# A graph layer with a layer norm on one core: column groups of 7, 1, 7, 1 blocks in place of 6, 2, 6, 2, one drained block a step, three raw slots in place of four

## The chip, the cores and the metric

The kernel runs on one core of a Trainium2 chip. The metric is device time in microseconds (us) of one execution; lower is better.

## The reference

With x of 8192 x 128, a dense adjacency matrix adj of 8192 x 8192, W of 128 x 128 and b of 128, all float32:

```python
h = jnp.maximum(_layernorm(x, axis=-1), 0.0)
support = jnp.matmul(h, W)
out = jnp.matmul(adj, support) + b
return x + jax.nn.relu(out)
```

The kernel computes it as (adj h) W: for each output column block it sums h-transposed times adj-transposed over all 8192 nodes and then projects the sum with W.

## The kernel before

**Tiling.** The output, transposed to 128 features x 8192 nodes, is cut into 16 column blocks of 512 (one PSUM bank each). The contraction runs over 64 k-tiles of 128 nodes. The blocks are done in four groups (WIDTHS, line 16): 6, 2, 6 and 2 blocks wide, on PSUM banks 0 to 5, 6 and 7, 0 to 5, 6 and 7. Group g takes all 64 k-tiles before group g+1 begins. A step handles DEPTHS[g] k-tiles of a group: 1 in the wide groups, 3 in the narrow ones, so nearly every step has six pairs of k-tile and block. There are 64 + 22 + 64 + 22 = 172 steps; the narrow groups begin at steps 64 and 150, the last of each has one k-tile.

**One step.** SP loads the step's part of adj into a slot of `raw` (line 270). ACT copies it to `high` in the rounded type fp32r (line 404). DVE writes `low` = raw - high, the rest that the rounding left (line 543). PE makes three fp32r products for each pair of k-tile and block (line 585): h_high x high, h_low x high, h_high x low. They are summed in the block's bank. Only the first two steps (FOUR_PASS, line 627) are plain float32 products straight from `raw`, since their h isn't split yet.

**Slots.** There are 4 of `raw`, 3 of `high`, 2 of `low`. SP's load of step t waits until DVE has made `low` of step t - 4 (line 297; for steps 4 and 5 until PE has used the raw slot, line 294). ACT's `high` of step t waits for `low` and the last use of `high` of step t - 3 (lines 399, 400). DVE's `low` of step t waits for PE's last product of step t - 2 (line 539). A step's load is cut into pieces of blocks (split_of, line 71): in group 0 [3, 3] or, in steps 2 to 23, [2, 2, 2]; elsewhere one piece of 1536 KB. ACT, DVE and PE go piece by piece. Each engine's instructions are written out in a fixed order: the loop over t on each engine is the queue.

**h.** During group 0 the layer norm of x is made in batches of four k-tiles beside the split of adj: DVE takes means and variances, ACT squares and rectifies (lines 369, 376), POOL makes z (line 347), DVE the low half (line 489).

**Draining.** When a group is complete its blocks leave PSUM during the next group. drained_at(t, after) names the block n for which step t is `after` steps behind its drain step (the group's first step + DRAIN_AT). At the drain step SP loads the block's residual x (load_residual, line 279), ACT copies the sum to `sum_high` (line 384) and DVE makes `sum_low` (line 498). One step later (PROJECT_AFTER) PE projects with three products (project, lines 611 to 613). Four later (FINISH_AFTER) DVE adds bias, relu and residual (finish, line 505). Nine later (STORE_AFTER) SP stores (line 283). POOL adds the bias to the residual (line 356). The residuals live in X_SLOTS = 4 slots of `x_sb`; load_residual(n) waits on SP until the store of block n - 4 has landed (line 278). With OUT_SLOTS = 2, ACT's sum_to_high waits for a projection two blocks back (line 383). A group that takes over banks waits on PE for output_ready (line 639).

**End.** In the last two steps PE finishes block 14, then block 15 (lines 691 to 700). It projects block 14 while ACT copies block 15 out of PSUM (line 423), then projects block 15 in two float32 halves (line 706). DVE finishes them (line 513), SP and ACT store them.

Of the kernel before, what the change touches and what calls it, by code (L numbers as in the profile page):

```python
# [6 lines left out]
P = 128  # L7
BANK = 512
N = 8192
TILES = N // P  # L10
COL_BLOCKS = N // BANK
# [1 line left out]

WIDTHS = [6, 2, 6, 2]
DEPTHS = [1, 3, 1, 3]
FIRST_BLOCK = [0, 6, 8, 14]
FIRST_BANK = [0, 6, 0, 6]
STEPS = [-(-TILES // d) for d in DEPTHS]  # L20
FIRST_STEP = [sum(STEPS[:g]) for g in range(len(WIDTHS))]
ALL_STEPS = sum(STEPS)
LAST = ALL_STEPS - 1

RAW_SLOTS, HIGH_SLOTS, LOW_SLOTS = 4, 3, 2
WIDEST = max(w * d for w, d in zip(WIDTHS, DEPTHS)) * BANK


# [5 lines left out]

FOUR_PASS = 2

NARROW_UNTIL = 24

HALVED_SINGLY = range(4, 10)

LOW_AT_ONCE_UNTIL = 7
WARMING, WARM = 2, 448
X_SLOTS = 4
Z_SLOTS = 2


DRAIN_AT = [3, 6, 8, 11, 13, 16]
PROJECT_AFTER, FINISH_AFTER, STORE_AFTER = 1, 4, 9
OUT_SLOTS = 2
EPS = 1e-5  # L50

HALF = BANK // 2
# [18 lines left out]
def split_of(t):  # L71

    g = group_of(t)
    if t == 0:
        return [1, 1, 2, 2]
    if g == 0:
        return [3, 3] if t < FOUR_PASS or t >= NARROW_UNTIL else [2, 2, 2]
    return [1] * WIDTHS[g] if t == LAST else [WIDTHS[g]]


def blocks_of(t, i):
# [92 lines left out]
def gnn_layer(nc, x_batches, x_blocks, adj_piece, W, b, out_blocks):  # L174
    with ExitStack() as ctx:  # L175
        def sb(name, shape, dt=F32):
            return ctx.enter_context(nc.sbuf_tensor(name, shape, dt))

        def sem(name):
            return ctx.enter_context(nc.semaphore(name))  # L180
# [5 lines left out]
        h_low = sb("h_low", [P, TILES, P], F32R)  # L186
        x_sb = sb("x_sb", [P, X_SLOTS, BANK])
        z_sb = sb("z_sb", [P, Z_SLOTS, BANK])
        squares = sb("squares", [P, 4, P])
# [17 lines left out]
        last_sum = sb("last_sum", [P, BANK])  # L207
# [7 lines left out]
        res_landed = [sem(f"res_landed{s}") for s in range(X_SLOTS)]  # L215
# [33 lines left out]
        stored = [sem(f"stored{s}") for s in range(X_SLOTS)]  # L249
        block = ctx.enter_context(nc.Block())  # L250

        def columns(t):
            g = group_of(t)
# [5 lines left out]
        @block.sync  # L259
        def _(sp):  # L260
            def load_x(j):

                if j == 5:
                    sp.wait_ge(centred, EARLY)
                if j > 5:
                    sp.wait_ge(z_ready, BATCHES[j - X_SLOTS][1] - EARLY)
                sp.dma_start(x_sb[:, x_slot(j), :], x_batches[j]).then_inc(x_landed[x_slot(j)], 16)  # L267

            def load_piece(t, i):
                sp.dma_start(raw[:, t % RAW_SLOTS, columns_of(t, blocks_of(t, i))], adj_piece(t, i)) \  # L270
                  .then_inc(raw_landed[t % RAW_SLOTS][i], 16)

            def load_residual(n):
                if n < X_SLOTS:

                    sp.wait_ge(z_ready, TILES - EARLY)
                else:
                    sp.wait_ge(stored[n % X_SLOTS], 16 * (n // X_SLOTS))
                sp.dma_start(x_sb[:, n % X_SLOTS, :], x_blocks[n]).then_inc(res_landed[n % X_SLOTS], 16)

            def store(n):
                sp.wait_ge(output_ready, n + 1)
                sp.dma_start(out_blocks[n], x_sb[:, n % X_SLOTS, :]).then_inc(stored[n % X_SLOTS], 16)

            sp.dma_start(x_sb[:, 0, 0:P], x_batches[0]).then_inc(x_first_landed, 16)  # L285

            for i in (0, 2, 3):
                load_piece(0, i)
            for t in range(1, ALL_STEPS):
                if t == 2:  # L290
                    load_x(3)
                if RAW_SLOTS <= t < RAW_SLOTS + FOUR_PASS:

                    sp.wait_ge(products_done, t - RAW_SLOTS + 1)
                if t >= RAW_SLOTS + FOUR_PASS:

                    sp.wait_ge(low_ready, halved(t - RAW_SLOTS))
                for i in range(len(split_of(t))):
                    load_piece(t, i)
                if mean_at(t) is not None:  # L300
                    load_x(mean_at(t))
                if t == 30:
                    sp.dma_start(W_sb[:, :], W).then_inc(params_landed, 16)
                    sp.dma_start(bias[:, :], b).then_inc(params_landed, 16)
                n = drained_at(t, 0)
                if n is not None:
                    load_residual(n)
                n = drained_at(t, STORE_AFTER)
                if n is not None:
                    store(n)  # L310
            for n in range(FIRST_BLOCK[-1], COL_BLOCKS):
                load_residual(n)
# [4 lines left out]
            for n in range(FIRST_BLOCK[-1], COL_BLOCKS - 1):  # L317
                store(n)
            n = COL_BLOCKS - 1
            sp.wait_ge(output_ready, n + 1)  # L320
            sp.dma_start(out_blocks[n][:, 0:HALF], x_sb[:, n % X_SLOTS, 0:HALF]).then_inc(stored[n % X_SLOTS], 16)
            for s in range(X_SLOTS):

                sp.wait_ge(stored[s], 16 * (COL_BLOCKS // X_SLOTS + (s == n % X_SLOTS)))

        @block.gpsimd
        def _(pool):
# [24 lines left out]
            nc.gpsimd.tensor_scalar(neg_bias[:, :], bias[:, :], -1.0, None, ALU.mult).then_inc(neg_bias_ready, 1)  # L352
            for n in range(COL_BLOCKS):

                pool.wait_ge(res_landed[n % X_SLOTS], 16 * (n // X_SLOTS + 1))
                nc.gpsimd.tensor_scalar(x_sb[:, n % X_SLOTS, :], x_sb[:, n % X_SLOTS, :], bias[:, 0:1], None,  # L356
                                        ALU.add).then_inc(x_biased, 1)

        @block.scalar
        def _(act):  # L360
# [55 lines left out]
                    sum_to_high(n)  # L416
            n = COL_BLOCKS - 1
            act.wait_ge(closing_products, 1)
            sum_to_high(n - 1)
            act.wait_ge(closing_products, 2)  # L420
            for half in range(2):
                cols = slice(half * HALF, (half + 1) * HALF)
                nc.scalar.activation(last_sum[:, cols], banks[:, bank_of(n), cols],
                                     ACT.Copy).then_inc(last_sum_ready, 1)
            act.wait_ge(output_ready, n + 2)
            act.dma_start(out_blocks[n][:, HALF:BANK], x_sb[:, n % X_SLOTS, HALF:BANK]) \
               .then_inc(stored[n % X_SLOTS], 16)

        @block.vector
        def _(dve):  # L430
# [71 lines left out]
            def finish(n):  # L502
                dve.wait_ge(x_biased, n + 1)
                dve.wait_ge(projected, n + 1)
                nc.vector.scalar_tensor_tensor(x_sb[:, n % X_SLOTS, :], banks[:, bank_of(n), :], neg_bias[:, 0:1],  # L505
                                               x_sb[:, n % X_SLOTS, :], ALU.max, ALU.add) \
                  .then_inc(output_ready, 1)

            def finish_last(half):
                n = COL_BLOCKS - 1  # L510
                cols = slice(half * HALF, (half + 1) * HALF)
                dve.wait_ge(last_projected, half + 1)
                nc.vector.scalar_tensor_tensor(x_sb[:, n % X_SLOTS, cols], banks[:, half, 0:HALF],  # L513
                                               neg_bias[:, 0:1], x_sb[:, n % X_SLOTS, cols],
                                               ALU.max, ALU.add).then_inc(output_ready, 1)

            for cols in (slice(0, P), slice(P, WARM)):
# [53 lines left out]
                        dve.wait_ge(neg_bias_ready, 1)  # L571
                    finish(n)
            n = COL_BLOCKS - 1
            sum_to_low(n - 1)
            finish(n - 1)
            dve.wait_ge(x_biased, n + 1)
            finish_last(0)
            finish_last(1)
# [2 lines left out]
        def _(pe):  # L581
# [49 lines left out]
            for t in range(FOUR_PASS, LAST - 1):  # L631
# [2 lines left out]
                opens, closes = s == 0, s == STEPS[g] - 1  # L634
                depths = range(depth_of(t))
                parts = parts_of(t)
                if opens and g >= 2:

                    pe.wait_ge(output_ready, FIRST_BLOCK[g - 1])

                def with_high(part):
                    pe.wait_ge(high_ready, halved(t, part))
                    if part == 0:
                        high_is_there(t)
                    for k in depths:
# [42 lines left out]
                    project(n)  # L688


            for c in range(WIDTHS[-1]):
                for t in (LAST - 1, LAST):
                    pe.wait_ge(high_ready, halved(t, c if t == LAST else None))
                    for h in (h_high, h_low):
                        for k in range(depth_of(t)):
                            product(t, c, k, h, high, t % HIGH_SLOTS)
                    pe.wait_ge(low_ready, halved(t, c if t == LAST else None))
                    for k in range(depth_of(t)):
                        last = product(t, c, k, h_high, low, t % LOW_SLOTS, stop=t == LAST and k == depth_of(t) - 1)
                last.then_inc(closing_products, 1)  # L700
            project(COL_BLOCKS - 2)
            pe.wait_ge(output_ready, FIRST_BLOCK[-1])
            for half in range(2):

# [43 lines left out]
```

## Time and profile before

| | us |
|---|---|
| median of 3 runs | 722.32 |
| the runs | 722.05, 722.32, 796.1 |
| the profiled execution, its own time | 721.9 |
| its span, first to last instruction | 720.1 |

The profiler takes one execution. Its span leaves out 1.8 us around the first and last instruction. The profiled execution stands 0.4 us under the median. PE is TensorE's matmul row and PEld its weight loads, DVE VectorE, ACT ScalarE, POOL GpSimd, SP the engine that issues most DMAs; a q behind a name (SPq, DVEq) is that engine's sequencer. A busy PE is not PE at its peak, as matmuls are pipelined: the pace is read from the starts of many matmuls in a row.

### The profile page before, as it was taken

The numbers are of one execution on the slowest core, as the hardware profiler recorded it, in microseconds if no ns is written. First come the engines' busy times: TensorE is split into PE (matmuls) and PEld (weight loads), VectorE is DVE, ScalarE is ACT, GpSimd is POOL, SyncE is SP. The second block draws the span as 40 slices with busy tenths as digits, with TensorE's granted clock in tenths as the row PEclk, the third lists the DMA queues.
The fourth block names the chain that finished last, engine by engine and source line by source line (L and its number), as shares of the span: only waits on it lengthen the run. The fifth ranks groups of instructions, "written<-read, shape, count | busy, mean of one in ns | idle before, by whom it ended". The sixth has DMA issues, their size and how long they took to land.

```text
span 720.1 us, 7905 instructions
## 1 busy us (share of the span) xinstructions
PE 715.2 (99%) x3113; PEld 583.8 (81%) x3113; DVE 623.3 (87%) x394; ACT 517.5 (72%) x400; POOL 181.4 (25%) x99
## 2 busy tenths in 40 slices
PE   9999999999999999999999999999999999999998
PEld 4878888888888888888888888888888888888886
DVE  5999999999999888988798888878788887888895
ACT  2788888888888767766577667667676676767662
POOL 4445555556544402410041000000000000033023
PEclk9999999999999999999999999999999999999999
DMA  9999999999999999999999999999999999999992
GB/s 353 408 408 409 409 411 415 412 415 416 417 415 414 418 421 407 415 387 404 359 410 428 383 402 396 364 397 386 379 390 391 382 391 385 398 403 397 389 382 77
DMA packets 45110, 281.60 MB, mean 391 GB/s; under 512 B 5137, under 2 KB 5777, under 8 KB 31505
## 3 DMA queue, kind: packets, MB, share of 16 engines
q1 hardware_dynamic: 44496, 280.25, 97.2%
q10 hardware_dynamic: 576, 0.85, 0.4%
q8 instruction: 24, 0.39, 0.2%
q14 instruction: 14, 0.11, 0.0%
HBM read 276.89 MB, written 4.19 MB: 390 GB/s over the span
## 4 chain that ended last, share of the span: by engine, by line
PE 94%; DMA 3%; DVE 1%; SPq 0%; ACT 0%; issue 0%; DVEq 0%; ACTq 0%
PE banks L585 93%; DMA raw<-adj 3%; DVE low L543 1%; PE banks L612 0%; PE banks L613 0%; PE banks L611 0%; SPq L270 0%; ACT high L404 0%; DVE h_low L489 0%; DVE x_sb L505 0%; DVE x_sb L513 0%; SPq L267 0%; DVEq L175 0%; SPq L285 0%; ACTq L403 0%
## 5 line engine op out<-in xcount | busy, mean ns | idle before, releaser
L543 DVE TENSOR_TENSOR low<-raw,high 128x3072 fp32r<-128x3072 f32 (+3 forms) x261 | 576.5, 2235 | 83.1 <-PE banks L585 69.9
L404 ACT ACTIVATE high<-raw 128x3072 fp32r<-128x3072 f32 (+3 forms) x261 | 483.6, 1864 | 188.6 <-DMA raw<-adj 160.7
L585 PE MATMUL banks<-high,h_high 128*128 128x512 f32 x1012 | 272.7, 390 | 0.1
L585 PE MATMUL banks<-high,h_low 128*128 128x512 f32 x1012 | 272.0, 389 | 0.0
L585 PE MATMUL banks<-low,h_high 128*128 128x512 f32 x1012 | 268.5, 389 | 0.0
L585 PEld LDWEIGHTS banks<-high,h_high 128*128 128x128 f32 x1012 | 189.6, 188 | 41.1 <-ACT high L404 1.6
L585 PEld LDWEIGHTS banks<-low,h_high 128*128 128x128 f32 x1012 | 189.7, 188 | 40.1 <-DVE low L543 0.8
L585 PEld LDWEIGHTS banks<-high,h_low 128*128 128x128 f32 x1012 | 190.0, 188 | 39.5
L356 POOL TENSOR_SCALAR x_sb<-x_sb,bias 128x512 f32<-128x512 f32 x16 | 54.5, 3409 | 414.2 <-DMA x_sb<-x_blocks 414.2
L347 POOL TENSOR_SCALAR z_sb<-x_sb,neg_mean,rstd 128x128 f32<-128x128 f32 x60 | 94.7, 1590 | 1.6
L332 POOL TENSOR_TENSOR rstd<-var_eps,minus_half 128x4 f32<-128x4 f32 (+2 forms) x17 | 31.6, 1860 | 112.8 <-DVE var_eps L447 103.6
L369 ACT ACTIVATE squares<-x_sb,neg_mean 128x128 f32<-128x128 f32 x52 | 20.1, 387 | 0.0
L384 ACT ACTIVATE sum_high<-banks 128x512 fp32r<-128x512 f32 x15 | 8.7, 580 | 7.0 <-PE banks L585 7.0
L505 DVE SCALAR_TENSOR_TENSOR x_sb<-banks,neg_bias,x_sb 128x512 f32<-128x512 f32 x15 | 11.2, 744 | 2.2 <-PE banks L613 2.2
L498 DVE TENSOR_TENSOR sum_low<-banks,sum_high 128x512 fp32r<-128x512 f32 x15 | 10.3, 683 | 2.1 <-ACT sum_high L384 2.1
L627 PE MATMUL banks<-raw,h_first 128*128 128x512 f32 x24 | 11.1, 607 | 0.2
L489 DVE SCALAR_TENSOR_TENSOR h_low<-z_sb,h_high 128x512 fp32r<-128x512 f32 x15 | 10.3, 690 | 0.0
L627 PEld LDWEIGHTS banks<-raw,h_first 128*128 128x128 f32 x24 | 4.2, 189 | 7.5 <-issue 4.5
L369 ACT ACTIVATION_READ_ACCUMULATOR squares<-x_sb,neg_mean 128x1 f32 x52 | 9.8, 188 | 0.0
L376 ACT ACTIVATE h_high<-z_sb 128x512 fp32r<-128x512 f32 x15 | 9.2, 614 | 0.0
L436 DVE TENSOR_REDUCE neg_sum<-x_sb 128x4 f32<-128x512 f32 x13 | 8.8, 674 | 0.0
L458 DVE BATCH_NORM_STATS2 stats<-x_sb 128x6 f32<-128x128 f32 x12 | 2.7, 282 | 4.4 <-DMA x_sb<-x 4.4
(34 smaller groups left out, 47.8 us busy)
## 6 DMA issues: line engine op xcount, KB each, us to landing
raw<-adj SPq DMA_DIRECT2D x106, 1536.0 KB, 8.6
raw<-adj SPq DMA_DIRECT2D x82, 768.0 KB, 10.6
raw<-adj SPq DMA_DIRECT2D x69, 512.0 KB, 11.9
x_sb<-x_blocks SPq DMA_DIRECT2D x16, 256.0 KB, 8.4
out_blocks<-x_sb SPq DMA_DIRECT2D x15, 256.0 KB, 8.7
x_sb<-x SPq DMA_DIRECT2D x14, 256.0 KB, 12.2
raw<-adj SPq DMA_DIRECT2D x3, 256.0 KB, 6.5
raw<-adj ACTq DMA_DIRECT2D x1, 256.0 KB, 2.8
```

Of the source, the lines that this page charges most:

```text
L332: nc.gpsimd.tensor_tensor(rstd[:, first:end], var_eps[:, first:end], minus_half[:, first:end], ALU.pow).then_inc(rstd_ready, 1)
L347: nc.gpsimd.tensor_scalar(z_sb[:, x_slot(j) % Z_SLOTS, cols], x_sb[:, x_slot(j), cols], neg_mean[:, t:t + 1], rstd[:, t:t + 1], ALU.add, A ...
L356: nc.gpsimd.tensor_scalar(x_sb[:, n % X_SLOTS, :], x_sb[:, n % X_SLOTS, :], bias[:, 0:1], None, ALU.add).then_inc(x_biased, 1)
L369: nc.scalar.activation(squares[:, before % 4, :], x_sb[:, x_slot(j), cols], ACT.Square, bias=neg_mean[:, t:t + 1], accum_out=sum_squares[: ...
L376: nc.scalar.activation(h_high[:, first:end, :], z_sb[:, x_slot(j) % Z_SLOTS, :].rearrange("p (t d) -> p t d", d=P), ACT.Relu).then_inc(h_h ...
L404: nc.scalar.activation(high[:, t % HIGH_SLOTS, cols], raw[:, t % RAW_SLOTS, cols], ACT.Copy).then_inc(high_ready, 1)
L489: nc.vector.scalar_tensor_tensor(h_low[:, first:end, :], z_sb[:, x_slot(j) % Z_SLOTS, :] .rearrange("p (t d) -> p t d", d=P), 0.0, h_high[ ...
L498: nc.vector.tensor_tensor(sum_low[:, n % OUT_SLOTS, :], banks[:, bank_of(n), :], sum_high[:, n % OUT_SLOTS, :].bitcast(F32), ALU.subtract) ...
L505: nc.vector.scalar_tensor_tensor(x_sb[:, n % X_SLOTS, :], banks[:, bank_of(n), :], neg_bias[:, 0:1], x_sb[:, n % X_SLOTS, :], ALU.max, ALU ...
L543: nc.vector.tensor_tensor(low[:, t % LOW_SLOTS, cols], raw[:, t % RAW_SLOTS, cols], high[:, t % HIGH_SLOTS, cols].bitcast(F32), ALU.subtra ...
L585: return nc.tensor.matmul(banks[:, FIRST_BANK[g] + c, :], h[:, (t - FIRST_STEP[g]) * DEPTHS[g] + k, :], tile[:, slot, at:at + BANK], start ...
L627: last = nc.tensor.matmul(banks[:, FIRST_BANK[0] + c, :], h_first[:, t, :], raw[:, t, c * BANK:(c + 1) * BANK], start=t == 0, stop=False)
```

## The change

The groups become 7, 1, 7 and 1 blocks wide, on banks 0 to 6, 7, 0 to 6, 7. A narrow step has six k-tiles of one block (64 = 10 x 6 + 4, so 11 steps, the last with four k-tiles). There are 64 + 11 + 64 + 11 = 150 steps; the narrow groups begin at steps 64 and 139. A wide step is 7 blocks (1792 KB), split [4, 3], in steps 2 to 19 of group 0 [3, 2, 2]; a narrow step stays at 1536 KB in one piece. `raw` has 3 slots. A block is drained on each of the steps 1 to 7 of the next group, projected 1 step later, finished 3 later and stored 6 later, with three OUT_SLOTS. The residuals have six slots, of which two are the home of z. On SP the store stands ahead of load_residual in a step. On PE the wait for free banks is now made part by part. The last group holds block 15 alone, so block 14 is projected eight steps ahead of the end's last two.

```diff
-WIDTHS = [6, 2, 6, 2]
-DEPTHS = [1, 3, 1, 3]
-FIRST_BLOCK = [0, 6, 8, 14]
-FIRST_BANK = [0, 6, 0, 6]
+WIDTHS = [7, 1, 7, 1]
+DEPTHS = [1, 6, 1, 6]
+FIRST_BLOCK = [0, 7, 8, 15]
+FIRST_BANK = [0, 7, 0, 7]
...
-RAW_SLOTS, HIGH_SLOTS, LOW_SLOTS = 4, 3, 2
+RAW_SLOTS, HIGH_SLOTS, LOW_SLOTS = 3, 3, 2
...
-NARROW_UNTIL = 24
+NARROW_UNTIL = 20
...
+RES_SLOTS = 6
...
-DRAIN_AT = [3, 6, 8, 11, 13, 16]
-PROJECT_AFTER, FINISH_AFTER, STORE_AFTER = 1, 4, 9
-OUT_SLOTS = 2
+DRAIN_AT = [1, 2, 3, 4, 5, 6, 7]
+PROJECT_AFTER, FINISH_AFTER, STORE_AFTER = 1, 3, 6
+OUT_SLOTS = 3
...
     if t == 0:
-        return [1, 1, 2, 2]
+        return [1, 1, 2, 3]
     if g == 0:
-        return [3, 3] if t < FOUR_PASS or t >= NARROW_UNTIL else [2, 2, 2]
-    return [1] * WIDTHS[g] if t == LAST else [WIDTHS[g]]
+        return [4, 3] if t < FOUR_PASS or t >= NARROW_UNTIL else [3, 2, 2]
+    return [4, 3] if g == 2 else [1]
...
+        def residual(n):
+
+            slot = n % RES_SLOTS
+            return x_sb[:, slot, :] if slot < X_SLOTS else z_sb[:, slot - X_SLOTS, :]
...
+                elif n < RES_SLOTS:
+
+                    sp.wait_ge(h_low_ready, TILES - EARLY)
                 else:
-                    sp.wait_ge(stored[n % X_SLOTS], 16 * (n // X_SLOTS))
-                sp.dma_start(x_sb[:, n % X_SLOTS, :], x_blocks[n]).then_inc(res_landed[n % X_SLOTS], 16)
+                    sp.wait_ge(stored[n % RES_SLOTS], 16 * (n // RES_SLOTS))
+                sp.dma_start(residual(n), x_blocks[n]).then_inc(res_landed[n % RES_SLOTS], 16)
...
+                n = drained_at(t, STORE_AFTER)
+                if n is not None:
+                    store(n)
                 n = drained_at(t, 0)
                 if n is not None:
                     load_residual(n)
-                n = drained_at(t, STORE_AFTER)
-                if n is not None:
-                    store(n)
...
             act.wait_ge(closing_products, 1)
-            sum_to_high(n - 1)
-            act.wait_ge(closing_products, 2)
...
-            sum_to_low(n - 1)
-            finish(n - 1)
...
-                if opens and g >= 2:
-
-                    pe.wait_ge(output_ready, FIRST_BLOCK[g - 1])
 
                 def with_high(part):
                     pe.wait_ge(high_ready, halved(t, part))
+                    if opens and g >= 2:
+
+                        pe.wait_ge(output_ready, FIRST_BLOCK[g - 2] + parts[part][1][-1] + 1)
...
-            project(COL_BLOCKS - 2)
             pe.wait_ge(output_ready, FIRST_BLOCK[-1])
```

## Rows read from the trace of the kernel before

**Rows 1.** The page: busy us of each engine; granted TensorE clock in 40 slices.

```profile
PE 715.2 (99%) x3113; PEld 583.8 (81%) x3113; DVE 623.3 (87%) x394; ACT 517.5 (72%) x400; POOL 181.4 (25%) x99
PEclk9999999999999999999999999999999999999999
```

**Rows 2.** The chain that ended last: start us, us, what, matmuls.

```profile
37.99 252.48 PE banks L585 x1112
...
312.30 0.23 PE banks L611
312.53 0.24 PE banks L612
312.77 0.23 PE banks L613
313.00 12.25 PE banks L585 x54
```

**Rows 3.** Waits of DVE and SP over the span: total us, times, longest.

```profile
DVE low L543 <- PE banks L585: 69.9, 89, 2.9
...
SPq L270 <- DVE low L543: 544.9, 162, 4.8
SPq L279 <- DMA out_blocks<-x_sb: 23.4, 5, 4.8
```

**Rows 4.** Groups of instructions by shape, whole span: busy us, mean ns.

```profile
L543 DVE TENSOR_TENSOR low<-raw,high 128x3072 fp32r<-128x3072 f32 x106 | 356.2, 3363 | 69.4 <-PE banks L585 63.8 <-ACT high L404 4.2
L404 ACT ACTIVATE high<-raw 128x3072 fp32r<-128x3072 f32 x106 | 294.6, 2779 | 139.5 <-DMA raw<-adj 115.7 <-PE banks L585 14.4 <-DVE low L543 9.3
L543 DVE TENSOR_TENSOR low<-raw,high 128x1536 fp32r<-128x1536 f32 x80 | 139.3, 1771 | 8.8 <-PE banks L585 6.1 <-ACT high L404 2.2
L404 ACT ACTIVATE high<-raw 128x1536 fp32r<-128x1536 f32 x80 | 118.1, 1486 | 23.6 <-DMA raw<-adj 23.4
L505 DVE SCALAR_TENSOR_TENSOR x_sb<-banks,neg_bias,x_sb 128x512 f32<-128x512 f32 x15 | 11.2, 744 | 2.2 <-PE banks L613 2.2
L498 DVE TENSOR_TENSOR sum_low<-banks,sum_high 128x512 fp32r<-128x512 f32 x15 | 10.3, 683 | 2.1 <-ACT sum_high L384 2.1
```

**Rows 5.** Start of the kernel: timelines of PE and of ACT.

```profile
4.69 11.19 PE L627 MATMUL banks<-raw,h_first 128*128 128x512 f32 x24
15.34 1.00 PE L585 MATMUL banks<-high,h_high 128*128 128x512 f32 x2
...
14.23 1.06 ACT L404 ACTIVATE high<-raw 128x1024 fp32r<-128x1024 f32 x1 [12.01 <-DMA raw<-adj]
```

**Rows 6.** Stretches: busy us of each engine, clock, DMA share, GB/s.

```profile
4.69:15.34 10.65, 10.53 (x24) 4.20 (x24) 6.29 (x37) 1.06 (x1) 4.46 (x7) 1.00 1.03 413
60.00:140.00 80.00, 80.00 (x354) 66.23 (x353) 77.41 (x75) 69.72 (x99) 44.73 (x26) 1.00 1.02 411
380.00:390.00 10.00, 10.00 (x45) 8.26 (x45) 8.80 (x5) 7.90 (x4) 2.89 (x1) 1.00 1.00 424
```

**Rows 7.** Loads of adj from issue to landing: 400:600, then 330:345, then 60:260.

```profile
DMA to landing us min/median/max: 7.3/8.4/10.2
...
DMA to landing us min/median/max: 5.8/8.3/8.5
...
DMA to landing us min/median/max: 7.9/11.1/13.3
```

**Rows 8.** SP's timeline around the first store and the residual load behind it.

```profile
302.77 0.33 SPq L270 DMA_DIRECT2D raw<-adj  x1
303.14 0.43 SPq L283 DMA_DIRECT2D out_blocks<-x_sb  x1
306.85 0.33 SPq L270 DMA_DIRECT2D raw<-adj  x1
311.89 0.33 SPq L279 DMA_DIRECT2D x_sb<-x_blocks  x1
```

**Rows 9.** The end: timeline of PE, ACT and DVE.

```profile
715.10 0.39 PE L611 MATMUL banks<-sum_high,W_high 128*128 128x512 f32 x1
715.30 0.66 ACT L423 ACTIVATE last_sum<-banks 128x256 f32<-128x256 f32 x2 [2.13 <-PE banks L585]
715.83 1.10 PE L706 MATMUL banks<-last_sum,W_sb 128*128 128x256 f32 x4
716.07 0.75 DVE L505 SCALAR_TENSOR_TENSOR x_sb<-banks,neg_bias,x_sb 128x512 f32<-128x512 f32 x1 [2.17 <-PE banks L613]
716.74 0.87 DVE L513 SCALAR_TENSOR_TENSOR x_sb<-banks,neg_bias,x_sb 128x256 f32<-128x256 f32 x2
```

More of the change, by code:

```diff
@@ L188, in gnn_layer @@
         z_sb = sb("z_sb", [P, Z_SLOTS, BANK])
-        squares = sb("squares", [P, 4, P])
+        squares_sb = sb("squares", [P, BANK])
+        squares = squares_sb[:, :].rearrange("p (t d) -> p t d", d=P)
         neg_sum = sb("neg_sum", [P, TILES])
@@ L206, in gnn_layer @@
         neg_bias = sb("neg_bias", [P, 1])
[L207 removed]
+        last_sum = squares_sb
         warm = last_sum[:, 0:WARM]
@@ L214, in gnn_layer @@
         x_first_landed = sem("x_first_landed")
-        res_landed = [sem(f"res_landed{s}") for s in range(X_SLOTS)]
+        res_landed = [sem(f"res_landed{s}") for s in range(RES_SLOTS)]
         params_landed = sem("params_landed")
@@ L248, in gnn_layer @@
         output_ready = sem("output_ready")
-        stored = [sem(f"stored{s}") for s in range(X_SLOTS)]
+        stored = [sem(f"stored{s}") for s in range(RES_SLOTS)]
         block = ctx.enter_context(nc.Block())
+        def residual(n):
+            slot = n % RES_SLOTS
+            return x_sb[:, slot, :] if slot < X_SLOTS else z_sb[:, slot - X_SLOTS, :]
         def columns(t):
@@ L276, in load_residual @@
                     sp.wait_ge(z_ready, TILES - EARLY)
-                else:
-                    sp.wait_ge(stored[n % X_SLOTS], 16 * (n // X_SLOTS))
-                sp.dma_start(x_sb[:, n % X_SLOTS, :], x_blocks[n]).then_inc(res_landed[n % X_SLOTS], 16)
+                elif n < RES_SLOTS:
+                    sp.wait_ge(h_low_ready, TILES - EARLY)
+                else:
+                    sp.wait_ge(stored[n % RES_SLOTS], 16 * (n // RES_SLOTS))
+                sp.dma_start(residual(n), x_blocks[n]).then_inc(res_landed[n % RES_SLOTS], 16)
             def store(n):
                 sp.wait_ge(output_ready, n + 1)
-                sp.dma_start(out_blocks[n], x_sb[:, n % X_SLOTS, :]).then_inc(stored[n % X_SLOTS], 16)
+                sp.dma_start(out_blocks[n], residual(n)).then_inc(stored[n % RES_SLOTS], 16)
             sp.dma_start(x_sb[:, 0, 0:P], x_batches[0]).then_inc(x_first_landed, 16)
@@ L307, in _ @@
                     load_residual(n)
-                n = drained_at(t, STORE_AFTER)
-                if n is not None:
-                    store(n)
-            for n in range(FIRST_BLOCK[-1], COL_BLOCKS):
-                load_residual(n)
+            load_residual(COL_BLOCKS - 1)
             for t in range(ALL_STEPS, ALL_STEPS + STORE_AFTER):
@@ L316, in _ @@
                     store(n)
-            for n in range(FIRST_BLOCK[-1], COL_BLOCKS - 1):
-                store(n)
             n = COL_BLOCKS - 1
             sp.wait_ge(output_ready, n + 1)
-            sp.dma_start(out_blocks[n][:, 0:HALF], x_sb[:, n % X_SLOTS, 0:HALF]).then_inc(stored[n % X_SLOTS], 16)
-            for s in range(X_SLOTS):
-                sp.wait_ge(stored[s], 16 * (COL_BLOCKS // X_SLOTS + (s == n % X_SLOTS)))
+            sp.dma_start(out_blocks[n][:, 0:HALF], residual(n)[:, 0:HALF]).then_inc(stored[n % RES_SLOTS], 16)
+            for s in range(RES_SLOTS):
+                sp.wait_ge(stored[s], 16 * (len(range(s, COL_BLOCKS, RES_SLOTS)) + (s == n % RES_SLOTS)))
         @block.gpsimd
@@ L353, in _ @@
             for n in range(COL_BLOCKS):
-                pool.wait_ge(res_landed[n % X_SLOTS], 16 * (n // X_SLOTS + 1))
-                nc.gpsimd.tensor_scalar(x_sb[:, n % X_SLOTS, :], x_sb[:, n % X_SLOTS, :], bias[:, 0:1], None,
+                pool.wait_ge(res_landed[n % RES_SLOTS], 16 * (n // RES_SLOTS + 1))
+                nc.gpsimd.tensor_scalar(residual(n), residual(n), bias[:, 0:1], None,
                                         ALU.add).then_inc(x_biased, 1)
@@ L425, in _ @@
             act.wait_ge(output_ready, n + 2)
-            act.dma_start(out_blocks[n][:, HALF:BANK], x_sb[:, n % X_SLOTS, HALF:BANK]) \
-               .then_inc(stored[n % X_SLOTS], 16)
+            act.dma_start(out_blocks[n][:, HALF:BANK], residual(n)[:, HALF:BANK]) \
+               .then_inc(stored[n % RES_SLOTS], 16)
         @block.vector
@@ L504, in finish @@
                 dve.wait_ge(projected, n + 1)
-                nc.vector.scalar_tensor_tensor(x_sb[:, n % X_SLOTS, :], banks[:, bank_of(n), :], neg_bias[:, 0:1],
-                                               x_sb[:, n % X_SLOTS, :], ALU.max, ALU.add) \
+                nc.vector.scalar_tensor_tensor(residual(n), banks[:, bank_of(n), :], neg_bias[:, 0:1],
+                                               residual(n), ALU.max, ALU.add) \
                   .then_inc(output_ready, 1)
@@ L512, in finish_last @@
                 dve.wait_ge(last_projected, half + 1)
-                nc.vector.scalar_tensor_tensor(x_sb[:, n % X_SLOTS, cols], banks[:, half, 0:HALF],
-                                               neg_bias[:, 0:1], x_sb[:, n % X_SLOTS, cols],
+                nc.vector.scalar_tensor_tensor(residual(n)[:, cols], banks[:, half, 0:HALF],
+                                               neg_bias[:, 0:1], residual(n)[:, cols],
                                                ALU.max, ALU.add).then_inc(output_ready, 1)
@@ L688, in _ @@
                     project(n)
[L691 to L697, printed above, removed]
-                    for k in range(depth_of(t)):
-                        last = product(t, c, k, h_high, low, t % LOW_SLOTS, stop=t == LAST and k == depth_of(t) - 1)
-                last.then_inc(closing_products, 1)
-            project(COL_BLOCKS - 2)
+            for t in (LAST - 1, LAST):
+                pe.wait_ge(high_ready, halved(t))
+                for h in (h_high, h_low):
+                    for k in range(depth_of(t)):
+                        product(t, 0, k, h, high, t % HIGH_SLOTS)
+                pe.wait_ge(low_ready, halved(t))
+                for k in range(depth_of(t)):
+                    last = product(t, 0, k, h_high, low, t % LOW_SLOTS, stop=t == LAST and k == depth_of(t) - 1)
+            last.then_inc(closing_products, 1)
             pe.wait_ge(output_ready, FIRST_BLOCK[-1])
```

## The prediction

> **What bounds the kernel now.** I read the page first. PE is busy 99% of the span at full clock in all slices, DVE 87%, ACT 72% [rows 1]. A busy PE is no proof that PE is the bound, so the chain that ended last comes next: from 37.99 us to the end it is PE alone, 1112 matmuls in one piece and pieces of 54 between the projections [rows 2]. 54 matmuls take 12.25 us, 0.227 us each, in every such piece. Counting the work gives the floor: 1024 pairs of k-tile and block, 12 of them in float32. 1012 x 3 x 0.227 = 688.7 us, the float32 ones fill 4.69 to 15.34 us (10.65 us, 12 products) [rows 5], and 15 projections of 3 matmuls add 10.2 us. That is 709.6 us of work between 4.69 and about 715.8 us [rows 9], 711.1 us. PE loses some 1.5 us in all. No regrouping of blocks takes a product away, so the change can win next to nothing; the question is what it costs.
>
> Behind PE stand two others with little room. DMA is at a share of 1.02 and 411 GB/s in group 0 [rows 6], and ACT waits for it all through [rows 4]. Those waits cost nothing: DVE waits behind ACT for PE 89 times, 69.9 us [rows 3], so the data is early. SP's waits for `low` (544.9 us) are its way of waiting for a free raw slot [rows 3]. That a slot comes free late is what the change makes likelier.
>
> **The change part by part.**
>
> *PE's work.* Two first steps of 7 blocks make 14 float32 products in place of 12. One costs 10.65 / 12 = 0.89 us [rows 5], an fp32r triple 3 x 0.227 = 0.68 [rows 2]: 2 x 0.21 = +0.4 us. The numbers of other products and projections stay.
>
> *Start.* PE reaches step 2 at 15.34 us, just as ACT's first `high` of it (1.06 us from 14.23) is ready [rows 5]: DMA, PE and ACT meet there. After the change three more blocks of 256 KB stand ahead of that point, 786 KB at 413 GB/s [rows 6] = 1.9 us, and the piece is 3 blocks, 1.49 in place of 1.06 us of ACT [rows 4, 5]: ready at 15.3 + 2.3 = 17.6. PE is there at 15.34 + 2 x 0.89 = 17.1. +0.5 us. The third raw slot missing does no harm yet: step 3's load waits for PE's step 0, over near 11 us, when load 2 is still moving.
>
> *Wide steps.* PE takes 21 x 0.227 = 4.77 us a step. DVE takes for [4, 3] some 2.30 + 1.77 = 4.1 us (the first from the rows for 3 and 6 blocks, 1.04 us a thousand columns) [rows 4], and the layer norm 0.4 us a step (77.41 us busy in 19.6 steps of 60:140, 3.95, less two pieces of 1.77) [rows 4, 6]: 4.5 of 4.77, where now it is 3.95 of 4.08. DVE gains room. The bytes for each PE second are the same, 385 GB/s, with x 399 in group 0; DMA has carried 424 [rows 6]. The loop of a raw slot is landing, ACT's and DVE's last piece (1.49 + 1.77), and it has 3 x 4.77 = 14.3 us, so a load may take 11.0 us from issue to landing. A one-piece load takes 8.4 us now [rows 7]; by bytes, x 7/6 = 9.8 us. It fits: 0 us. Group 0's 11.1 us (up to 13.3) [rows 7] are the other bound; they come with DMA saturated and four slots queued, and fewer slots shorten a queue. I take 0, and keep the other for a rival.
>
> *Narrow steps.* A step is 4.08 us, 4.76 with a projection; 7 of the 11 have one. DVE takes 3.36, with sum_low and finish 3.36 + 0.68 + 0.74 = 4.79 us [rows 4] in the four steps that have both: even with PE, no longer below it. The slot's loop is landing + 2.78 + 3.36 us [rows 4]. Plain steps give it 12.24 us, hence 6.1 us for a landing, drain steps 14.3, hence 8.1. The rows say 8.4 in the median, and 5.8 at the least, where DMA had run dry [rows 7]. With 8.4 a slot comes back 0.1 us late a step in drain steps, 0.8 in plain ones. Against this stands the stock: DVE now ends `low` 0.7 us before PE starts the step (it waits for PE, then takes 3.36 of 4.08), and PE needs `low` only 12 matmuls, 2.7 us, into the step. That is 3.4 us to lose before PE stops.
>
> *SP's queue, the dearest part.* At step 7 of a narrow group SP loads the step, stores block 0 (8 in the second), and then load_residual(6) (14) waits until that same store has landed, since 6 slots behind is the block just stored. finish(0) comes on DVE behind `low` of step 4 and a sum_low, 1.4 us after the `low` that let SP on. The store goes behind a full load: now a store at 303.14 releases SP at 311.89, 8.8 us later [rows 8]; with less queued between 6 and 8.8. SP is free 7.5 to 10.2 us after `low` of step 4, but the load of step 8 is due 4.8 us after it: 2.7 to 5.4 us late. Behind SP's wait stands nothing but these loads; ACT, DVE and PE wait for them. Landing 5.8 to 6.5 us later (DMA has run dry, residual ahead) instead of 8.4 gives back 2; so the raw data is 1 to 4 us late, with a slack of 1.0 (DVE would have waited for PE) and the 3.4 of stock, of which about 1 is used up by the late loop. The rest is a stall of PE of 0 to 1.5 us, and perhaps again in step 9, when stores add 256 KB (0.6 us) a step. Two groups: 0 to 3 us, say 1.5. Stores and residuals else are hidden: SP has until the next `low`. The wait for banks, by parts, is met: finish(6) is in step 10, the group ends with it.
>
> *End.* Project(14) now fills the 0.7 us in which ACT copies block 15; PE starts the last projection at 715.83, when both are over [rows 9]. After, the same 0.7 us stand ahead of the last product and the copy is bare: +0.7. DVE's finish(14) (716.07 to 716.74) no longer delays the two last halves: -0.2 [rows 9]. +0.5 us.
>
> Sum: 721.9 (the profiled execution's own time) + 0.4 + 0.5 + 0.5 + 1.5 = 724.8; the median of the runs is 0.4 above that execution, so 725.2 us.
>
> **A rule beside a row.** The quickest 1536 KB load lands in 5.8 us [rows 7]. The Trainium skill ("DMA: Bandwidth & Descriptors", Anatomy of one DMA) fits a GpSimd-issued DMA with about 2.0 us plus bytes over 436 GB/s, which is 5.6 us here, an estimate by that page; the row agrees, for a lone load. By it no narrow step would be late, and the stalls vanish (723.7 us); the medians of 8.4 us speak against it as a rule for loads that overlap.
>
> **The rivals.**
>
> A, *nothing is late*: with three slots fewer loads overlap, landings shrink toward 5.8 us [rows 7], and the stock covers SP's wait. For it: PE stopped nowhere in the five such waits now, of up to 4.8 us [rows 3]; against it, those had a fourth slot. The time is 725.2 - 1.5 = 723.7 us.
>
> B, *the narrow groups run short*: landings stay at 8.4 us and the store takes its full 8.8. Then each group loses the 4 us of SP's lateness, 0.8 in each of three plain steps and 0.6 in each of three steps with a store, less 4.4 of slack and stock: about 3.8 us. Twice, 7.6 us: 731.3 us.
>
> C, *the other side, slower by over 2%*: three slots don't carry the wide groups. It decides from a landing of 11.0 us: each us above it costs a third of a us a step. If group 0's 11.1 to 13.3 us [rows 7] stay as they are, at 12 it is 0.33 x 128 steps = 43 us, 766 us; at 11.4 it would be 17 us, about 741 us. Against it: with 5.5 MB in three slots and 400 GB/s a slot turns over in 13.7 us at the DMA's own pace, so a long landing is a queue, and no queue means a short one.
>
> **How the numbers follow.** Chances: the forecast (short stalls of PE, 724.4 to 727) 0.42, A 0.31, B 0.20, C 0.06; a gain of over 2% would need 14.4 us where PE loses 1.5 in all, 0.01. The range reaches from just under A (722.8, if the start or the end costs nothing) to B (731.5). 2% (14.4 us) is about what a measurement can tell from no change: all but C lie within it. Faster 0.01, same 0.93, slower 0.06.
>
> **What would show it.** The profile after should have PE in one piece in both wide groups, with DVE still waiting for PE there; at steps 7 and 8 of the narrow groups a wait of SP on line 279's store of several us, then ACT waiting for raw and a gap of PE under 2 us; first fp32r product near 17.6 us. Landings in the wide groups under 11 us show that C is out, landings near 6 us in the narrow ones that A is right. The forecast is wrong if PE waits in the wide groups, or if gaps stand where SP did not wait for a store.

## The result, and the profile after

The changed kernel takes 734.18 us in the median of 4 runs (731.77 to 734.92), against 722.36 us before: a ratio of 1.0164, 95% interval 1.0151 to 1.0176. It is 11.8 us slower. One execution of the kernel before, at 796.1 us, is far above its others and counts as slow, so the ratio leaves it out. Forecast were 725.2 us and a range to 731.5. The profiled execution is the quickest of the four, 731.77 us, so some 2.4 us of the median have to be looked for outside it.

The page of the kernel after: span, busy us, the granted clock, DMA rate in 40 slices.

```profile
span 730.0 us, 7969 instructions
...
PE 718.3 (98%) x3111; PEld 584.6 (80%) x3111; DVE 620.9 (85%) x431; ACT 516.1 (71%) x437; POOL 174.0 (24%) x99
...
PEclk9999999999999999999999999999999999999999
...
GB/s 357 411 412 411 411 418 412 417 409 393 418 418 412 405 397 384 377 386 266 352 423 420 420 418 389 379 392 396 377 384 395 377 385 396 385 382 370 358 329 194
```

PE, one piece before [rows 1, 2], has less of its span; one slice of DMA, the 19th (328 to 347 us), falls to 266 GB/s, and at the end there are 329 and 194. The chain that ended last says what lies there (start us, us, what; pieces of issue and of queue time between them are left out):

```profile
18.20 281.19 PE banks L588 x1239
...
299.41 3.97 DVE low L548 x2
...
303.40 8.72 DMA raw<-adj
...
315.10 3.37 DVE low L548
...
318.48 8.81 DMA raw<-adj
...
334.92 8.44 DMA out_blocks<-x_sb
...
343.37 0.33 SPq L289
...
343.74 8.38 DMA raw<-adj
...
352.22 2.77 ACT high L411
...
383.55 276.10 PE banks L588 x1218
...
694.61 8.01 DMA out_blocks<-x_sb
...
703.01 6.76 DMA raw<-adj
```

Both wide groups are still PE alone, 281 and 276 us in one piece. Each narrow group is a loop of landing, ACT, DVE, landing; and then SP stands behind its own store for 8 us (line 289 is load_residual), in both groups. PE in the first narrow group, steps 71 and 72 (steps 7 and 8 of the group):

```profile
345.64 1.65 PE L588 MATMUL banks<-high,h_high 128*128 128x512 f32 x6
...
349.10 1.68 PE L588 MATMUL banks<-low,h_high 128*128 128x512 f32 x6 [0.46 <-DVE low L548]
...
355.04 2.04 PE L588 MATMUL banks<-high,h_high 128*128 128x512 f32 x6 [3.56 <-ACT high L411]
356.88 2.77 PE L588 MATMUL banks<-high,h_low 128*128 128x512 f32 x6
```

PE stands still for 3.56 us. Six products then take 2.77 us where they take 1.52 elsewhere. The stretches of the same kernel tell why (busy us of each engine, granted clock, DMA share, GB/s):

```profile
352.00:356.00 4.00, 0.96 (x4) 0.83 (x5) 0.91 (x1) 2.76 (x1) 0.00 (x0) 1.00 1.01 421
356.00:360.00 4.00, 4.00 (x12) 3.13 (x12) 3.95 (x3) 2.79 (x2) 0.00 (x0) 0.57 0.74 232
```

In the four us behind the idle stretch the granted clock is 0.57 in the mean, most of it at the lower of the two levels, 1.2 in place of 2.4 GHz. From the start of step 71 (345.64) step 72 should begin 4.8 us later, at 350.4; it begins at 355.04, 4.6 us late, and itself takes 6.5 us (to 361.57) in place of 4.8. So the first narrow group costs 6.3 us. Of the last 1.7 not all is the clock: DVE ends `low` of step 72 only at 358.45, 3.4 us into the step, where PE at full clock wants it after 2.7. The same step of the second group, behind a gap of 1.64 us and at full clock, takes 5.7 us (712.70 to 718.36). So the clock's part in this execution is some 0.8 to 0.9 us. The second group costs 2.7 in the same reckoning (gaps of 1.64 and 0.39 us). With 1.4 us for start and end this is 10.4, where the two profiled executions are 9.9 apart.

### The profile page after: what moved, and what is told of

Same layout as the page of the kernel before. It is cut to its first block, busy times and chain, and to the rows that moved or that the text cites. A ratio compares the mean times of both kernels' runs of the same rounds, so it can differ in the third digit from the quotient of the medians.

```text
span 730.0 us, 7969 instructions
## 1 busy us (share of the span) xinstructions
PE 718.3 (98%) x3111; PEld 584.6 (80%) x3111; DVE 620.9 (85%) x431; ACT 516.1 (71%) x437; POOL 174.0 (24%) x99
## 4 chain that ended last, share of the span: by engine, by line
PE 83%; DMA 10%; DVE 3%; ACT 2%; issue 1%; SPq 0%; DVEq 0%; ACTq 0%
PE banks L588 81%; DMA raw<-adj 8%; DVE low L548 3%; ACT high L411 2%; DMA out_blocks<-x_sb 2%; PE banks L630 1%; DVE sum_low L503 0%; DVE x_sb L510 0%; SPq L277 0%; PE banks L616 0%; PE banks L615 0%; PE banks L614 0%; PE banks L707 0%; SPq L289 0%; DVE x_sb L518 0%
## 5 line engine op out<-in xcount | busy, mean ns | idle before, releaser
L548 DVE TENSOR_TENSOR low<-raw,high 128x1536 fp32r<-128x1536 f32 (+4 forms) x298 | 574.2, 1966 | 95.6 <-ACT high L411 47.4
L411 ACT ACTIVATE high<-raw 128x1536 fp32r<-128x1536 f32 (+4 forms) x298 | 480.9, 1650 | 203.0 <-DMA raw<-adj 184.1
L588 PE MATMUL banks<-high,h_high 128*128 128x512 f32 x1010 | 278.5, 390 | 5.2 <-ACT high L411 5.2
L588 PE MATMUL banks<-high,h_low 128*128 128x512 f32 x1010 | 278.6, 390 | 0.0
L588 PE MATMUL banks<-low,h_high 128*128 128x512 f32 x1010 | 275.0, 390 | 0.8 <-DVE low L548 0.8
L363 POOL TENSOR_SCALAR x_sb<-x_sb,bias 128x512 f32<-128x512 f32 x12 | 32.8, 2731 | 388.6 <-DMA x_sb<-x_blocks 388.6
L354 POOL TENSOR_SCALAR z_sb<-x_sb,neg_mean,rstd 128x128 f32<-128x128 f32 x60 | 100.1, 1680 | 1.6
L630 PE MATMUL banks<-raw,h_first 128*128 128x512 f32 x28 | 12.8, 602 | 0.7 <-DMA raw<-adj 0.7
L363 POOL TENSOR_SCALAR z_sb<-z_sb,bias 128x512 f32<-128x512 f32 x4 | 10.5, 2616 | 9.9 <-DMA z_sb<-x_blocks 9.9
L510 DVE SCALAR_TENSOR_TENSOR x_sb<-banks,neg_bias,x_sb 128x512 f32<-128x512 f32 x11 | 8.2, 743 | 0.0
```

What stands on the lines that cost most here:

```text
L354: nc.gpsimd.tensor_scalar(z_sb[:, x_slot(j) % Z_SLOTS, cols], x_sb[:, x_slot(j), cols], neg_mean[:, t:t + 1], rstd[:, t:t + 1], ALU.add, A ...
L363: nc.gpsimd.tensor_scalar(residual(n), residual(n), bias[:, 0:1], None, ALU.add).then_inc(x_biased, 1)
L411: nc.scalar.activation(high[:, t % HIGH_SLOTS, cols], raw[:, t % RAW_SLOTS, cols], ACT.Copy).then_inc(high_ready, 1)
L548: nc.vector.tensor_tensor(low[:, t % LOW_SLOTS, cols], raw[:, t % RAW_SLOTS, cols], high[:, t % HIGH_SLOTS, cols].bitcast(F32), ALU.subtra ...
L588: return nc.tensor.matmul(banks[:, FIRST_BANK[g] + c, :], h[:, (t - FIRST_STEP[g]) * DEPTHS[g] + k, :], tile[:, slot, at:at + BANK], start ...
L630: last = nc.tensor.matmul(banks[:, FIRST_BANK[0] + c, :], h_first[:, t, :], raw[:, t, c * BANK:(c + 1) * BANK], start=t == 0, stop=False)
```

## The experiments

The kernel before was timed beside each group of runs: 722.01, 721.72 and 721.9 us.

**SP's wait for its own store, taken away.**

```diff
+AFTER_STORE = (6, 14)
...
-                if n is not None:
+                if n is not None and n not in AFTER_STORE:
+                    load_residual(n)
+                n = drained_at(t, 2)
+                if n in AFTER_STORE:
                     load_residual(n)
```

> The changed kernel with one edit: the residual loads of blocks 6 and 14 are issued two steps later (step 9 of the narrow group in place of step 7), when the store that frees their slot has long landed. SP no longer waits the 8 us on its own store. Theory S (SP's wait in front of the load of step 8 starves PE, and each starved stretch lowers the granted clock after it): no gap of PE over 1 us is left in either narrow group, only some tenths from raw slots that come back late; granted clock 1.000; 724 to 726 us. Theory L (the three-slot loop alone runs PE dry in the narrow groups, the store is a bystander): the gaps move to the next steps and stay 3 us and more a group; 730 us and more.

Measured: 726.99 us (726.01 to 728.07), ratio 1.0069 (1.0054 to 1.0084). 7.2 us are back, and 5.0 are left. The waits of PE for ACT and DVE in this kernel:

```profile
PE banks L592 <- DVE low L552: 1.4, 4, 0.5
```

No gap is over 0.5 us, as theory S has it; theory L's gaps of 3 us don't come. The time is 1 us above S's range. The chain still goes through the slots' loop in both narrow groups, and PE stops there for some tenths, 1.4 us in all; that is about half of the 2.7 us by which this span (724.2 us) exceeds that of the kernel with both edits below (721.5 us).

**The three slots' loop, shortened.** ACT and DVE work on each narrow step in two halves, loaded in one piece. PE may then also begin a step on the first half.

```diff
+    if DEPTHS[group_of(t)] > 1:
+        return [(0, range(0, 1), range(0, 3)), (0, range(0, 1), range(3, depth_of(t)))]
...
+                if DEPTHS[g] > 1:
+                    with_high(0)
+                    with_high(1)
+                    with_low(0)
+                    with_low(1)
```

> The changed kernel, but ACT and DVE split each narrow step in two halves of three k-tiles (one load as before); PE takes both halves' high products, then both halves' low products. DVE's second half ends 1.77 us after ACT's second, so the slot's loop is shorter by some 1.3 us in each of 20 steps; two more DVE and ACT instructions a step cost 0.1 to 0.2 us each. SP's wait stays. Theory S: less stock is used up before step 8, so PE's gaps shrink from 4.3 and 2.0 us to about 3 and 1; 728 to 730 us. Theory L: the gaps are mostly gone, 725 us.

Measured: 726.14 us (724.5 to 727.07), ratio 1.0055 (1.004 to 1.007). That is better than the 728 to 730 of S and close to L's 725. SP still waits, and PE hardly does:

```profile
SPq L296 <- DMA out_blocks<-x_sb: 16.5, 3, 7.9
...
PE banks L595 <- DVE low L555: 0.6, 2, 0.3
...
PE banks L595 <- ACT high L418: 0.3, 1, 0.3
```

So neither theory stands by itself: SP's 8 us are bearable where the loop has not yet used up the stock, and the loop is bearable where SP doesn't stand still. That PE may begin on the first half isn't what saved step 72: ACT had both halves ready at 350.1 us, and PE came to the step at 350.42.

**Both together.**

> Both edits of the two runs before it: residual loads of blocks 6 and 14 two steps later, and narrow steps in two halves on ACT and DVE. Both theories: no gap of PE over 0.5 us in the narrow groups, granted clock 1.000, and what is left over the kernel before is the start (+0.9 us: two more float32 products and ACT's larger first piece) and the end (+0.5 us): 723.5 to 724.5 us. If it is well above, something else than the narrow groups is slower.

Measured: 723.0 us (722.35 to 725.15, 10 runs), ratio 1.0014 (1.0005 to 1.0023). As expected, and its span of 721.5 us is 1.4 above the 720.1 before. In its chain PE goes from 20.20 us without a break:

```profile
20.20 306.31 PE banks L599 x1350
```

Each edit alone brings 7 to 8 us, both 11.2, not 15: most of the stall needs both causes, and taking away either one removes it. What is left is start and end.

**Three slots in the kernel before**, RAW_SLOTS = 3 and nothing else.

> The kernel before with three raw slots in place of four and nothing else. One-piece steps of 1536 KB then have 12.24 us for a landing and 6.14 us of ACT and DVE. Theory Q (a long landing is queueing, and shrinks toward 6 us when fewer loads overlap): landings of the one-piece groups fall to 6 or 6.5 us, 722 to 735 us. Theory F (a landing keeps its 8 us or so with only the next load beside it, since loads in flight share the DMA engines): 8.4 + 6.2 = 14.6 us a slot against 12.24 us, 0.8 us lost in each of the 108 one-piece steps, PE stopping in each: about 800 us, more if the granted clock falls.

Measured: 804.72 us (802.14 to 806.59), ratio 1.1154 (1.1136 to 1.1173). SP's loads of adj between 440 and 640 us, all one-piece steps, and the same stretch's busy times:

```profile
L270 SPq DMA_DIRECT2D raw<-adj x41: 327/328/328, 444.1 to 639.5; - x41
...
DMA to landing us min/median/max: 6.5/8.2/10.3
```
```profile
440.00:640.00 200.00, 179.95 (x735) 135.14 (x735) 137.91 (x42) 114.30 (x42) 0.00 (x0) 0.99 0.87 326
```

The landing stays at 8.2 us (8.4 before [rows 7]) though DMA is now at a share of 0.87 and 326 GB/s. Theory Q falls for one-piece loads of this size. The pace is 195.4 / 40 = 4.88 us a step; the loop is 8.2 + 2.78 + 3.36 = 14.3, with 0.2 us for the gaps between landing, ACT, DVE and the next issue 14.5, a third of which is 4.85.

**Is it the slots' bytes, or the work behind the landing?** Two ways to shorten that work in the kernel with three slots: load and work in two pieces, or load in one and work in two.

```diff
-    return [1] * WIDTHS[g] if t == LAST else [WIDTHS[g]]
+    return [WIDTHS[g] // 2] * 2
```

> The kernel before with three raw slots, and its one-piece steps (groups 1 to 3) loaded and worked on in two pieces of half the size. ACT's and DVE's work behind the last landing falls from 6.14 to 1.49 + 1.77 = 3.3 us. Theory M (a slot's loop is the landing plus this work, and PE is fed as long as it is under three steps, 12.24 us): 8.2 + 3.3 = 11.5 us fits, so the 83 us that three slots cost come back almost whole: 722 to 728 us. Theory N (three slots hold too few bytes for the DMA queue to keep its rate): still 750 us and more.

```diff
+    if len(parts) == 1:
+        half = WIDTHS[group_of(t)] // 2
+        return [(0, range(0, half)), (0, range(half, 2 * half))]
```

> The kernel before with three raw slots; steps are still loaded in one piece in groups 1 to 3, but ACT and DVE work on each in two halves. Theory M: the loop is 8.2 + 1.49 + 2 x 1.77 + 0.2 = 13.4 us against 12.24, 0.4 us lost in each of 108 steps: about 765 us, halfway between three slots (804.7) and two pieces. Theory N: as three slots alone, 800 us.

Measured: two pieces 724.52 us (722.83 to 727.24, 10 runs), ratio 1.0041 (1.0027 to 1.0056); halved work 767.15 us (762.61 to 773.85), ratio 1.0658 (1.0608 to 1.0708). In the second, SP's loads run from 439.7 to 637.0 us, and DVE waits for ACT about once a step, ahead of its first half:

```profile
L273 SPq DMA_DIRECT2D raw<-adj x45: 327/328/328, 439.7 to 637.0; - x45
...
DMA to landing us min/median/max: 6.3/8.2/10.5
```

197.3 / 44 = 4.48 us a step; the loop 8.2 + 1.49 + 3.54 + 0.2 = 13.4, a third of which is 4.48. Three kernels, three paces (4.88, 4.48, and PE's own 4.08 where the sum of 11.5 is below three steps), one sum, good to 0.03 us a step. Theory M stands, N falls: with two pieces the same three slots carry 393 GB/s from 440 to 640 us.

**Why did the load behind SP's wait land so late?** In the changed kernel it took 8.38 us, though DMA had run dry. First the next load is held back:

> The changed kernel; in step 9 of both narrow groups SP waits until the load of step 8 has landed before it issues the next load. So the load issued right behind SP's long wait (landing 8.4 us in the changed kernel although DMA had run dry) moves with only a residual of 256 KB ahead of it. Theory H (loads in flight share the engines, so the ones issued behind it stretched it): it lands in 5.6 to 6.5 us, and PE's gap at step 8 shrinks by 2 us; the next load then comes later, so the time is not the point. Theory G (a landing of a 1536 KB load is about 8 us whatever is beside it): 8 us and more again.

Then nothing is in front of it either (residual, store and next load come after its landing):

> The changed kernel; in step 7 of a narrow group SP waits for its store as before, but then issues the load of step 8 first, with nothing ahead of it, and waits for its landing before it issues the residual load, the store and the next load. DMA engines hold nothing else meanwhile. If what lies around the load in the queue stretched it (it took 8.4 us in the changed kernel and 8.5 us with the next load held back), it lands in 5.6 to 6 us. If a landing is 8 us by itself, it takes 8 us here too. The time is no matter: the loads behind come later, 735 us or more.

The first took 736.55 us (735.29 to 737.82), the second 735.95 us in its one run. SP's timelines, of the first (both narrow groups) and of the second. What waits for the landing is in the first the next load (at 352.98, and at 714.00), in the second the residual at 349.10:

```profile
344.05 0.33 SPq L289 DMA_DIRECT2D x_sb<-x_blocks  x1
344.43 0.43 SPq L277 DMA_DIRECT2D raw<-adj  x1
344.90 0.43 SPq L293 DMA_DIRECT2D out_blocks<-x_sb  x1
352.98 0.33 SPq L277 DMA_DIRECT2D raw<-adj  x1
...
706.94 0.43 SPq L277 DMA_DIRECT2D raw<-adj  x1
707.41 0.43 SPq L293 DMA_DIRECT2D out_blocks<-x_sb  x1
714.00 0.33 SPq L277 DMA_DIRECT2D raw<-adj  x1
```
```profile
342.86 0.33 SPq L277 DMA_DIRECT2D raw<-adj  x1
349.10 0.33 SPq L289 DMA_DIRECT2D x_sb<-x_blocks  x1
```

With a residual ahead and a store behind it the load took 8.5 us in the first narrow group and 7.0 in the second; alone it took 6.2 in both (the second 702.13 to 708.31). In the traces where the next load is not held back (the changed kernel and the filled one below, two of each) the same load took 8.4, 6.9, 8.0 and 8.6 us in the first group and 6.8, 6.6, 7.0 and 6.7 in the second. So holding back the next load changed nothing that stands out of that spread, and theory H had the wrong neighbour; theory G's 8 us whatever is beside it falls too. What the two 256 KB transfers cost is 0.4 to 2.4 us, where their bytes at 424 GB/s [rows 6] give 1.2. Which of the two it is, and why it is less than their bytes in one group and mostly more in the other, was not tried.

**The clock.** Unread products fill PE's gap without shortening it.

```diff
+FILLED = {72: (1, 14), 147: (9, 7)}
...
+                if t in FILLED:
+                    free, count = FILLED[t]
+                    pe.wait_ge(output_ready, free)
+                    for _ in range(count):
+                        nc.tensor.matmul(banks[:, 0, :], h_high[:, 8, :],
+                                         h_high[:, 8:12, :].rearrange("p t d -> p (t d)"), start=True, stop=True)
```

> The changed kernel with extra products that nobody reads put where PE stood idle: 14 (3.2 us) ahead of step 8 of the first narrow group, 7 (1.6 us) ahead of the same step of the second, into a bank that is free. They fill the gaps and don't shorten them. Theory K (an idle stretch of some us makes the chip grant a lower clock for a while after it, which is part of what a late load costs): the granted clock stays at 1.00, and the time falls by the 1 to 3 us of slowed matmuls, 731 to 732.5 us against 734.2. Theory J (the clock has no part in it): 734 us, or more where a filler is longer than its gap.

Measured: 732.43 us (729.2 to 733.19), ratio 1.0137 (1.0114 to 1.0161), which overlaps the changed kernel's. So both were timed again, on one chip:

> The changed kernel as it is, timed beside the filled one on the same chip. Theory K (the clock falls after an idle stretch): granted clock 0.993 to 0.998, 732 to 735 us, 1 to 3 us above the filled kernel. Theory J: the two agree.

> The filled kernel once more (14 unread products ahead of step 8 of the first narrow group, 7 of the second), beside the changed kernel on the same chip. Theory K: granted clock 0.999 or 1.000, 730 to 733 us, 1 to 3 us under the changed kernel. Theory J: the two agree.

| | mean granted clock of four executions | us |
|---|---|---|
| changed | 1.000, 0.993, 0.993, 0.995 | 731.03, 734.0, 734.19, 734.68 |
| filled | 1.000, 0.999, 1.000, 1.000 | 733.7, 731.54, 731.81, 731.04 |

The changed kernel: 734.09 us, ratio 1.0161 (1.014 to 1.0182). The filled: 731.68 us, ratio 1.0133 (1.0116 to 1.015). The intervals still touch, so the 2.4 us between the medians are not certain by the times alone. The clocks are: in eight filled executions of both runs it never fell under 0.999, of eight unfilled ones seven lie at 0.998 or below. The eighth (731.03 us, clock 1.000) was profiled. Its load of step 72 landed after 6.9 us, PE stood for 1.74 us in place of 3.56, and the clock did not fall; the step took 5.66 us (352.31 to 357.97):

```profile
352.31 1.69 PE L588 MATMUL banks<-high,h_high 128*128 128x512 f32 x6 [1.74 <-ACT high L411]
...
355.77 1.66 PE L588 MATMUL banks<-low,h_high 128*128 128x512 f32 x6 [0.39 <-DVE low L548]
...
357.97 1.53 PE L588 MATMUL banks<-high,h_high 128*128 128x512 f32 x6
```
```profile
356.00:360.00 4.00, 4.00 (x18) 3.25 (x18) 3.01 (x2) 3.18 (x2) 0.00 (x0) 1.00 0.91 316
```

And in the filled kernel the stretch that follows the place of the gap has full clock:

```profile
353.00:357.00 4.00, 4.00 (x19) 2.99 (x17) 3.47 (x2) 2.76 (x2) 0.00 (x0) 1.00 0.94 377
```

Held against the 0.57 of the changed kernel after its 3.56 us, and 0.50 (356 to 360 us) in the kernel with the next load held back, after a gap of 3.70 us, where the step took 7.5 us. Theory K stands for the clock: a long gap lowers it, and filling the gap prevents that. For the time it is likely and not shown: the medians are 2.4 us apart with intervals that touch, and the gap itself differs by nearly 2 us between two executions of one kernel.

None of these versions beats the kernel before.

## Why the prediction was wrong, point by point

*PE is the bound and can't win anything.* Right: with all stalls gone (both edits) the kernel is at 723.0 us, 1.0 above the one before.

*PE's work and the start, +0.9 us.* Right in size: the first fp32r product of step 2 comes at 17.77 us, forecast 17.6 (15.34 before [rows 5]). Small waits of PE for adj (0.7 us in all) lie in the first step.

*The end, +0.5 us.* Right. The last projection starts at 725.90, 0.95 us after the start of the last product, as before (715.83 [rows 9]), but project(14) now stands ahead of that product. In the kernel with both edits the spans differ by 1.4 us, which is start and end together, as forecast.

*Wide steps, 0.* Right, and so was the reason against rival C. DVE still waits for PE (47.2 us in all, 69.9 before [rows 3]), and with three slots group 0's landings fell, with pieces of other sizes in both groups. Loads of adj from issue to landing, 60:260 and 400:600, for 11.1 and 8.4 us in [rows 7]:

```profile
DMA to landing us min/median/max: 6.7/8.6/10.6
...
DMA to landing us min/median/max: 6.3/7.9/10.0
```

*Narrow steps: "about 1 us of the stock is used up".* This is the first term that failed. When DVE ends `low`, against the step's start on PE (0.5 us ahead of it in the kernel before, where DVE ends at 570.21 and PE starts at 570.73; the prediction had 0.7):

```profile
315.10 3.36 DVE L548 TENSOR_TENSOR low<-raw,high 128x3072 fp32r<-128x3072 f32 x1 [2.05 <-ACT high L411]
...
330.27 3.36 DVE L548 TENSOR_TENSOR low<-raw,high 128x3072 fp32r<-128x3072 f32 x1 [2.16 <-ACT high L411]
...
345.69 3.36 DVE L548 TENSOR_TENSOR low<-raw,high 128x3072 fp32r<-128x3072 f32 x1 [1.57 <-ACT high L411]
```

Steps 65, 68 and 71 share a slot. PE starts them at 317.57, 331.23 and 345.64, and `low` ends 0.9, 2.4 and 3.4 us after that: the whole stock is gone at step 71, and PE's 0.46 us there is a stall before SP's wait has any effect. That gap, with no wait of SP for a store before it, is the prediction's own sign of being wrong. A turn takes 8.8 + 2.78 + 3.36 us and 0.2 of hand-overs: 15.1 to 15.4 us in the three turns that end in steps 65, 68 and 71, by the ends of `low`. I had rightly set 8.4 + 6.14 against the time of three steps, but divided the shortfall as 0.1 us a step, because I took 14.3 us for every turn. These three have 13.6, 13.7 and 14.4 us, as each of the first two has one plain step of 4.08 us in it. So they lose 1.5, 1.5 and 1.0 us, 4.0 in all, where the prediction had about 1. The landing of 8.8 in place of 8.4 us and the hand-overs weren't in the sum.

*"A stall of PE of 0 to 1.5 us".* The sum is off in itself: 4 us late at most, less 1.0 of slack and 2.4 of stock left, is 0.6 us at step 8. The 1.5 us that went into the forecast, the middle of twice that range, was more than these terms give, and still far less than the 9.0 us (6.3 + 2.7) that came.

*SP's wait: "2.7 to 5.4 us late".* The mechanism and the place were right. The size was the upper bound: the load of step 72 goes out at 343.74, `low` of step 69 ended at 338.33, 5.4 us. The wait for the store behind it, SP's own, total, times, longest in the profile after:

```profile
SPq L289 <- DMA out_blocks<-x_sb: 16.2, 3, 8.1
```

*"Landing 5.8 to 6.5 us later instead of 8.4 gives back 2."* This failed. It took 8.38 us, 6.76 in the second group. One quick load in the trace [rows 7], 5.8 us, was read as what an empty DMA gives and called a lone load, and the residual and the store around the load of step 72 were left out. The quick load was neither: it went out at 342.34, and the share of DMA was 1.01, 0.93 and 0.81 in the two-us stretches from 342 to 348. Alone, the load takes 6.2 us. The Trainium skill's fit ("DMA: Bandwidth & Descriptors", Anatomy of one DMA; 2.0 us plus bytes over 436 GB/s, an estimate of 5.6 us) is near that lone 6.2, and no help for loads with company (6.6 to 8.6 us).

*A term that wasn't there: the clock.* I counted a gap of PE as its own length. It costs more: some 0.9 us after the 3.56 us in the profile (6.5 us for the step, against 5.7 at full clock), and 1.8 after the 3.70 us of the kernel with the next load held back. The sum of terms, redone with what was measured: 721.9 + 1.4 + 6.3 + 2.7 = 732.3 for the profiled 731.8. The 2.4 us from there to the median lie in executions that were not profiled. Their clocks are lower (0.997, 0.994 and 0.993 against 0.998), so part of it is likely the clock; how much, and how much is longer gaps, stays open.

*The rivals.* The case that came is B in place and cause. B's price was near for the profiled execution: 2 x 3.8 = 7.6 us for the two groups, measured 6.3 + 2.7 = 9.0, of which 0.9 are the clock. B had two equal groups, and 6.3 and 2.7 came. Its chance, 0.20, was low because I let the median landing of 8.4 us [rows 7] shrink where it suited: rival A's argument that fewer loads overlap. With three slots in the kernel before, it stayed at 8.2, and the seven loads from 303 to 334 us of the changed kernel took 8.8 in the median. The range ended where B's sum ended, with no room for what a stall starts.

## What to carry to other kernels

Write the loop of a buffer slot as a sum (landing by its median, each engine's work behind the last piece, hand-overs) and hold it against the time of the very steps that the turn spans; where it is longer, multiply by the turns and see when the stock is gone. Loading and working in two pieces is worth nearly as much as a fourth slot: it took 3 us from the sum and brought 80 of 83 us back. Don't let a queue wait for a store that it has issued just before; and when PE can run dry, price the gap with what the clock takes after it.

## What the runs showed of the hardware

- A load of 1536 KB took 8.2 us in the median with DMA at a share of 0.87, as it took 8.4 at 0.98. Alone it took 6.2 us (twice, one execution); with a 256 KB load just ahead and a 256 KB store just behind it, 6.6 to 8.6 us in ten cases of five executions (in eight of them with the next load behind it too).
- The granted clock fell after long gaps of PE: 0.57 and 0.50 over four us after 3.56 and 3.70 us (from 356 us in both), 0.66 after 3.77 us (720 to 724 us, lone load), 0.71 after 3.16 us (536 to 540 us, the kernel before with three slots). It was 1.00 after gaps of 1.67, 1.74 and 2.06 us, and after the place of a gap filled with products. The kernel before with three slots has 80 waits of PE, 46.7 us in all, of which the one of 3.16 us is the longest, and a mean clock of 0.998.
